# Order of two VectorE steps within a group of a graph attention kernel

## The reference

```python
score = (Kh[src] * Qh[dst] * (1.0 / np.sqrt(D)) * Ee).sum(-1)
score = jnp.exp(jnp.clip(score, -5.0, 5.0))
msg = Vh[src] * score[..., None]
wV = jax.ops.segment_sum(msg, dst, num_segments=n)
...
x = _layernorm(x + wV)
```

## Time and profile before

| | |
|---|---|
| Median of three runs | 2970.64 us |
| Span of the profiled execution, first to last instruction | 1658.6 us |
| Median less span | 1312.0 us |
| Mean granted TensorE clock in the span | 0.978 |
| Busy in the span: PE, DVE, POOL, ACT | 1575.1, 1434.6, 1217.4, 942.7 us |

### The profile page before, as it was taken

One profiled execution on the slowest core, in us unless ns is written; L12 is line 12 of the kernel. 1 busy time (PEld: TensorE's weight loads), 2 busy tenths in 40 slices (PEclk: granted clock), 3 DMA queues, 4 the chain that ended last, 5 costly groups with the idle time before them and its releaser, 6 DMA issues. The chain is left out here.

```text
span 1658.6 us, 58065 instructions
## 1 busy us (share of the span) xinstructions
PE 1575.1 (95%) x18046; PEld 1394.5 (84%) x18046; DVE 1434.6 (86%) x2542; ACT 942.7 (57%) x2857; POOL 1217.4 (73%) x1298
## 2 busy tenths in 40 slices
PE   6599999999999999999999999999999999999994
PEld 6588888888888888888888888888888888888884
DVE  6588888898898898888888888888889889889886
ACT  3455555555555555565565565555555555555553
POOL 6677777777777777777777777777777777777772
PEclk8799999999999999999999999999999999999995
DMA  9655555555555555555555555555555555555541
GB/s 303 165 142 143 139 137 145 141 138 139 146 140 136 141 147 138 136 150 136 139 146 138 137 142 139 140 139 137 142 142 139 135 146 141 136 138 148 137 125 50
DMA packets 197529, 236.36 MB, mean 143 GB/s; under 512 B 95864, under 2 KB 122592, under 8 KB 197312
## 3 DMA queue, kind: packets, MB, share of 16 engines
q1 hardware_dynamic: 156992, 152.99, 32.9%
q0 software_dynamic: 40512, 83.05, 21.4%
HBM read 228.46 MB, written 7.40 MB: 142 GB/s over the span
## 5 line engine op out<-in xcount | busy, mean ns | idle before, releaser
L293 POOL DMA_INDIRECT kv<-kv_table,idx x1266 | 1198.8, 947 | 400.8 <-issue 382.5
L744 PE MATMUL xg_bank<-x_hi,src_onehot 128*128 128x448 f32 x2422 | 902.6, 373 | 7.4 <-DVE src_onehot L882 0.9
L745 PE MATMUL xg_bank<-x_lo,src_onehot 128*128 128x448 f32 x2422 | 882.7, 364 | 0.0
L744 PEld LDWEIGHTS xg_bank<-x_hi,src_onehot 128*128 128x128 f32 x2422 | 454.3, 188 | 67.9 <-issue 15.3
L745 PEld LDWEIGHTS xg_bank<-x_lo,src_onehot 128*128 128x128 f32 x2422 | 454.8, 188 | 33.0
L821 ACT ACTIVATE distance<-iota_w,dst_neg 128x64 f32<-128x64 f32 x1612 | 428.5, 341 | 0.0
L882 DVE TENSOR_TENSOR src_onehot<-r_row,xg_bank 128x896 fp32r<-128x896 f32 x346 | 372.7, 1077 | 0.0
L894 DVE SCALAR_TENSOR_TENSOR x_sel<-iota_v,src_block,xg_bank 128x448 f32<-128x448 f32 x346 | 233.7, 676 | 24.5 <-PE xg_bank L745 21.2
L847 ACT COPY xg_t_sb<-turn_sum 128x128 f32<-128x128 f32 x198 | 52.9, 267 | 351.2 <-PE turn_sum L754 351.2
L900 DVE TENSOR_REDUCE xg_sb<-x_sel 128x64 f32<-128x448 f32 x346 | 214.5, 620 | 11.9
L928 DVE TENSOR_TENSOR kq<-kv,edge_ps 128x512 f32<-128x512 f32 x202 | 138.2, 684 | 96.8 <-ACT kv L854 92.0
(11 more groups left out here) (113 smaller groups left out, 904.2 us busy)
## 6 DMA issues: line engine op xcount, KB each, us to landing
attr_sb<-attr SPq DMA_DIRECT2D x201, 256.0 KB, 2.9
dst_row<-dst_rows SPq DMA_DIRECT2D x402, 128.0 KB
kv<-kv_table,idx POOLq DMA_INDIRECT x1266
r_row<-r_table SPq DMA_DIRECT2D x148, 128.0 KB
q_win<-q_table SPq DMA_DIRECT2D x404, 24.0 KB
idx<-src_tab SPq DMA_DIRECT2D x206, 4.0 KB, 4.1
r_row<-r_table SPq DMA_DIRECT2D x50, 64.0 KB
kv_table<-kv_stage SPq DMA_DIRECT2D x7, 448.0 KB, 7.8
```

The lines of the kernel that those rows point to most:

```text
L293: pool.indirect_dma_start(out=kv[:, slot, t, :], out_offset=None, in_=kv_table, in_offset=bass.IndirectOffsetOnAxis(ap=idx[:, slot, t:t + ...
L744: pe.matmul(xg, src_onehot[:, parity, u, :], x_hi[:, u, :], start=(u == 0), stop=False)
L745: mm = pe.matmul(xg, src_onehot[:, parity, u, :], x_lo[:, u, :], start=False, stop=(u == U - 1))
```

## The change

In L945 to L948 the two steps change places: VectorE first selects the second tile of group g + 1, then makes the second source one-hot of group g + 2. Both conditions hold in slots 3 and 0; in slot 1 only the selection is there, in slot 2 only the one-hot. The instructions and their waits are the same.

```diff
@@ -942,10 +942,10 @@
                         dve.wait_ge(score_summed, g + 1)
                         dve.tensor_scalar(score_c[slot % 2][:, 0:n * H], score[slot % 2][:, 0:n * H], -CLIP, CLIP,
                                           ALU.max, ALU.min).then_inc(score_clipped, 1)
+                        if pe_tiles(g + 1, (j + 1) % SLOTS) == 2:
+                            select_x(g + 1, i, j + 1, 1, odd)
                         if pe_tiles(g + 2, (j + 2) % SLOTS) == 2:
                             make_src_onehot(g + 2, i, j + 2, 1, odd)
-                        if pe_tiles(g + 1, (j + 1) % SLOTS) == 2:
-                            select_x(g + 1, i, j + 1, 1, odd)
                         dve.wait_ge(exp_made, g + 1)
```

## The result

The changed kernel took 2876.86 us in the median of five runs (2860.57 to 2885.65), the kernel before 2965.46 us in the same comparison (2953.63 to 2973.09): a ratio of 0.970, 95% interval 0.9668 to 0.9732 (a range behind a ratio is such an interval from here on). The forecast was 2955.7 us. It got the sign right and the size wrong: 89 us less instead of 15.

What follows compares the result with a forecast made beforehand. TensorE with VectorE (31.456 us a round) was taken as the bound, GpSimd (31.213 us) just behind and capping the gain: 2970.6 - 14.9 = 2955.7 us, range 2942 to 2976 us.

Steps and rivals of the forecast that it cites:

- the two paces: Round of four groups: TensorE and VectorE 31.456 us, GpSimd's 25 gathers 31.213 us; two nearly equal bounds, 0.8% apart.
- The turn's wait, 0.77 us a round: TensorE's turning matmul (L754) waiting for VectorE's selection in slots 3 and 0: 0.77 us saved per round, at least 0.45.
- The lead used up near group 65: GpSimd's 9.87 us lead over L928 shrinks 0.52 us a round; then L928 of slot 3 waits for gathers, rounds 31.21 us.
- the end from GpSimd alone: GpSimd's last gather sets the end: L928 of group 201 starts 14.9 us earlier, span 1643.7 us.
- the larger gaps of GpSimd: Longer gaps between GpSimd's gathers from about group 99, 6.0 us together, would go because slots are released earlier.
- the one on the 1312 us: Median is 1312 us above the profiled span, cause not in the profile; left unchanged, giving 2970.6 - 14.9 us.
- The near balance of 31.46 and 31.21 us: TensorE/VectorE and GpSimd round paces; said to leave the profiled execution no slack for slower loops or faster gathers.
- The rival "nothing arrives": Extra 1312 us inside the loops, perhaps low clock; selection done before the turn, swap changes nothing: 2970.6 us, chance 0.24.
- The rival "slower": Second gather_x waits for the one-hot made 1.4 us later, once L928 waits for gathers: 2983 us, chance 0.05.
- that the timed loops would run at 2.4 GHz too: From the skill's rule that activity releases the half clock: same work, so full clock in timed loops; used against "nothing arrives".

Runs made afterwards that it cites:

- before_less: Kernel before with one gather of slot 3 left out in 49 groups, fast chip: 1658.7 us, ratio 0.9994.
- after_less: Changed kernel with the same 49 gathers of slot 3 left out, fast chip: 1621.3 us, ratio 0.9771 to the kernel before.
- b_slow: Kernel before, unchanged, traced on slow chip 12: median 2961.6 us, profiled execution 2967.9 us with a span of 2966.1 us.
- few_mm: Kernel before without two of the three terms of the queries (L719: 8 matmuls instead of 24 a group), slow chip 12: 2631.6 us, ratio 0.8842.
- early_b: Second tile's selection moved ahead of L928 in slots 3, 0 and 1, without delays, slow chip 12: 3074.9 us, ratio 1.0372 to the kernel before.

## Why the prediction was right or wrong

*What bounds the kernel, the two paces.* Right for the kind of chip that the trace was taken on: before_less and after_less show both bounds separately, 37.9 us against 38 worked out.

*The turn's wait, 0.77 us a round.* Right there: rounds of 30.6 to 30.7 us in after_less against 30.69 worked out, with 31.46 before.

*The lead used up near group 65, the end from GpSimd alone.* Right there: 15.1 us measured for 14.9, and the wait for the gathers named in advance is in the trace, some ten groups late and not in slot 3 alone. Also the larger gaps of GpSimd went, as said. On slow chips this step does not hold: GpSimd, which was to set the time at both bounds, waits 1195.6 us for the messages in the changed kernel.

*The failed step is the one on the 1312 us.* "I leave it as it is" took the difference between median and span for time around the loops. It was inside them: in `b_slow`, as long as the timed executions, each round takes 57.7 us and not 31.46, and 1.8 us lie outside the span. The turn's wait that the change works on is 390.7 us there, where the sum had it at 22.4 us. A span of 56% of the median should have been read as a sign that the trace does not show the timed executions. The near balance of 31.46 and 31.21 us, which the prediction held against slower loops, is a fact of the profiled execution alone. The sum, right for that trace, said nothing on the timed executions. The sign was right because the turn waits for the selection on both kinds of chip, which the trace of before could not show, so in the forecast it was luck.

*The rival "nothing arrives" had the premise and not the consequence.* The time was inside the loops and the clock low, as it put it (mean 0.752 in the kernel before on chip 12). But the busy time of TensorE is not doubled: it grows from 1575 to 2167 us, by 592 us of the 1308, and the larger part is idle time. And it concluded that slower matmuls would cover VectorE's selection. ScalarE gets the projection up to 6.6 us late (medians of the slots), VectorE stands idle and then has its whole stretch from L928 to L900 exposed. TensorE's wait for the selection is 390.7 us there, not 22.4 us, and GpSimd, which took the gain on fast chips, waits 1313 us for messages. So the swap pays on both kinds, and six times as much on the slow one.

*The rival "slower"* needed TensorE to wait for the second one-hot. In the changed kernel it waits 0.2 us for one-hots on a fast chip and 1.1 us on a slow one, over the whole execution.

What is shown of the 89 us: the swap in slot 3 alone, where the one-hot stood in front of the selection that slot 0's turn waits for, gives 73 us, and the round's stretch from slot 3 to slot 0 shortens by 3.9 us while the next grows by 1.5. More than the one-hot's own 1 us was thus won in one place and some given back in the next. So the size of the gain on slow chips is measured but not explained. Why the copy of slot 0 then comes 1.7 us and not 6.6 us after its projection is not settled.

What makes a chip slow is narrowed down and not settled either: leaving out small TensorE instructions gives more than their own time there (few_mm), small matmuls stand 0.7 us apart (early_b), and the half clock comes with the pauses. Late handling of TensorE's instructions would fit all three, but only leaving instructions out was tried on a slow chip. It could not be told whether they are delivered late or their completion is passed on late.

The Trainium skill, "TensorE: Matmul & The Clock Gate", Part 1, has TensorE's clock released by activity. The traces agree in that the mean granted clock was 0.978 where TensorE was busy 95% of the span and 0.767 where it was 73%. What the prediction drew from it, that the timed loops would run at 2.4 GHz too, did not hold, since they had the same work but not the same pauses. The low clock is thus more likely a companion of the pauses than their cause, though no run separates the two.

## What to carry to other kernels

When the median and the span of the profiled execution differ by far more than the 2 us that they did in every execution here, suspect that the trace is of another situation than the timing. Before working out a sum, ask how the change fares where the loops themselves are slower, and give that case its own sum. An engine whose rows show a constant gap behind every instruction is a full queue, whatever its busy share says; its pace is read from start to start, and it caps what a shorter chain elsewhere can bring. In an order written out by hand, the step that another engine waits for goes first and the step with 2 us of cover behind it; that order was never worse here, on either kind of chip, while moving it further up, in front of a product that did not need it, cost 3.7 to 7.7%. Only where the copy in front of that product was held back artificially was the early place the best one.

## What was not expected of the hardware

- The same kernel took 1659 us on three chips and 2965 to 2989 us on two, steady within 1% on each in all but one run (3047 us on chip 12, at a mean granted clock of 0.594).
- On slow chip 12 TensorE matmuls of 64 columns stood, in some stretches, 0.7 us or a multiple apart (`early_b`), where 16 of them take 1.0 us on a fast one and, in other stretches, on the slow one too. ScalarE, idle and waiting for a TensorE result, went on up to 8.5 us after the matmul's recorded end (`b_slow`).
- 16 small matmuls (32 instructions) a group cost 0.18 us when added on a fast chip, and leaving out 16 gave 1.65 us (333 us over 202 groups) on a slow one.
- GpSimd's indirect gathers of 128 rows kept a distance of about 1.25 us on fast and slow chips when they did not wait (medians of 1.249 us in the kernel before on either kind and 1.252 us in the changed one on a slow chip), 0.94 to 0.95 us of it recorded as busy.
